# Selective-scan head loop of a macaron layer: each VectorE instruction waits for the matmul it needs instead of for the end of TensorE's slot

## The reference

```
x = x + 0.5 * ffn(layernorm(x))
x = x + attn(layernorm(x))          # attn: res + mamba2(ln1), then res + gelu-MLP(ln2)
x = x + 0.5 * ffn(layernorm(x))

# in mamba2: 32 heads of 64 channels, state 64 x 64 per head
def step(h, inp):
    x_t, dt_t, B_t, C_t = inp
    dA = exp(dt_t * A)
    h = h * dA[:, :, None, None] + (dt_t[:, :, None] * x_t)[..., None] * B_t[:, None, None, :]
    y = einsum('bhpn,bn->bhp', h, C_t)
    return (h, y)
y = ys + xs * D;  y = y * silu(z);  y = rmsnorm(y) * norm_w;  y @ out_proj_w.T
```

## Time and profile before

| quantity | value |
|---|---|
| median of four runs | 9365.92 us |
| the four runs | 9269.44, 9272.82, 9459.03, 9481.4 us |
| the profiled execution, its own time | 9273.08 us |
| span of its slowest core (core 3) | 9271.5 us |
| spans of the eight cores | 9232.7 to 9271.5 us |
| mean granted TensorE clock, as a share of 2.4 GHz | 0.710 to 0.711 on every core |

### The profile page before, as it was taken

How to read it: one execution, slowest core, us unless ns; L and a number is a source line. 1 busy time by engine, 2 the same in 40 slices (tenths; PEclk the granted TensorE clock), 3 DMA queues, 4 the chain that set the end, 5 groups by cost and what they waited for, 6 DMA issues and landing times.

```text
span 9271.5 us, 108299 instructions; the slowest of 8 cores (9232.7 to 9271.5 us)
## 1 busy us (share of the span) xinstructions
PE 5135.0 (55%) x22944; PEld 2260.1 (24%) x22944; DVE 4583.0 (49%) x12271; ACT 1898.0 (20%) x3892; POOL 60.0 (1%) x117
## 2 busy tenths in 40 slices
PE   0068888434434434335235335334337898888888
PEld 0023333212111212112112112112113343333333
DVE  2046656455555554554654654554552221365555
ACT  0023333211211211211112112112112222233332
POOL 1000000000000000000000000000000000000000
PEclk6589999655655656556557556556558999999999
DMA  9953433100100101001002002002004444434444
GB/s 184 204 147 117 126 121 117 58 1 12 52 1 23 40 1 37 27 1 57 7 1 63 1 1 63 1 1 63 1 1 125 136 134 137 125 121 130 129 127 126
DMA packets 191391, 653.06 MB, mean 70 GB/s; under 512 B 21296, under 2 KB 46128, under 8 KB 179504
## 3 DMA queue, kind: packets, MB, share of 16 engines
q1 hardware_dynamic: 174624, 590.46, 20.4%
q0 software_dynamic: 16176, 55.66, 4.1%
HBM read 629.62 MB, written 72.09 MB: 76 GB/s over the span
## 4 chain that ended last, share of the span: by engine, by line
PE 38%; DVE 35%; issue 14%; DMA 7%; ACT 3%; DVEq 2%; SPq 0%; ACTq 0%; POOL 0%; POOLq 0%
PE ps L242 38%; DVE arena L578 4%; DVE arena L573 4%; DVE arena L986 4%; DVE arena L769 4%; DVE hstate L997 3%; DVE arena L582 3%; DVEq L92 2%; DVE arena L960 2%; DVE arena L947 2%; DVE arena L968 2%; DVE arena L1072 1%; DMA cffn<-arena 1%; DMA arena<-wffn 1%; DMA arena<-wm 1%
## 5 line engine op out<-in xcount | busy, mean ns | idle before, releaser
L242 PE MATMUL ps<-arena,wk 128*128 128x512 f16 x15552 | 3542.7, 387 | 1080.2 <-DMA wk<-cffn 502.9
L242 PEld LDWEIGHTS ps<-arena,wk 128*128 128x128 f16 x15552 | 1511.9, 99 | 3103.7 <-issue 1436.5
L242 PE MATMUL ps<-arena 128*64 128x128 f16 (+1 forms) x1568 | 455.0, 290 | 1654.1 <-DVE arena L986 1311.5
L1010 ACT ACTIVATE arena<-arena 128x128 f32<-128x128 f32 x1024 | 316.5, 309 | 2762.4 <-DVE arena L947 2762.4
L947 DVE TENSOR_SCALAR arena<-ps,arena 128x128 f32<-128x128 f32 x1024 | 359.2, 351 | 853.6 <-PE ps L242 774.3
L573 DVE SCALAR_TENSOR_TENSOR arena<-arena,prm,ps 128x512 f32<-128x512 f32 x512 | 382.2, 747 | 636.8 <-ACT arena L571 547.7
L242 PEld LDWEIGHTS ps<-arena 128*64 128x64 f16 (+1 forms) x1568 | 198.7, 127 | 1917.7 <-issue 1859.1
L242 PE MATMUL ps<-arena,ind 32*128 32x128 f16 x3072 | 484.7, 291 | 283.1 <-issue 133.0
L568 ACT ACTIVATE arena<-ps,prm 128x512 f32<-128x512 f32 x512 | 351.9, 687 | 526.7 <-DVE arena L578 518.0
L578 DVE SCALAR_TENSOR_TENSOR arena<-arena,prm 128x512 f32<-128x512 f32 x512 | 384.4, 751 | 54.0 <-DVE arena L573 0.9
L249 PE MATMUL ps<-iden,arena 32*128 32x32 f32 x96 | 15.9, 287 | 703.5 <-DVE arena L811 703.5
(11 more groups left out here) (117 smaller groups left out, 3458.7 us busy)
## 6 DMA issues: line engine op xcount, KB each, us to landing
wk<-cffn SPq DMA_DIRECT2D x512, 512.0 KB, 3.9
wk<-cm SPq DMA_DIRECT2D x256, 512.0 KB, 3.7
wk<-cip SPq DMA_DIRECT2D x136, 512.0 KB, 3.6
wk<-cop SPq DMA_DIRECT2D x64, 512.0 KB, 3.8
arena<-wffn POOLq DMA_DIRECT2D x16, 1024.0 KB, 15.0
cffn<-arena SPq DMA_DIRECT2D x16, 1024.0 KB, 9.2
arena<-wm POOLq DMA_DIRECT2D x16, 1024.0 KB, 12.9
cm<-arena SPq DMA_DIRECT2D x16, 1024.0 KB, 4.8
```

Source lines behind the costliest of these rows:

```text
L242: e.matmul(a, l, r, start=st, stop=sp, tile_position=tp),
L1010: sD[s] = B.E("s", lambda e, s=s: e.activation(Dex[s % 2], e1[s % 2], AF.Exp), waits=[(s_v, ve1[s])], inc=s_s)
```

## The change

TensorE's counter is noted at four more places: after D(s) as `tD[s]`, after the transpose as `tTR[p]`, after Y(hh) as `tY[hh]` and after H(p) as `tH[p]`. VectorE's instructions no longer wait for `tslot[s]` but for the value that belongs to what they read. Where an instruction overwrites a buffer that an earlier matmul reads, and `tslot` had covered this, a wait for that matmul is added. Two waits of TensorE's transposes for `dx` of the chunk before are new as well. No engine's instructions change their order or their number, waits apart.

```diff
+                        tD[s] = s_t.n
...
+                        elif vdx_prev.get(p + 14) is not None:
+                            w0.append((s_v, vdx_prev[p + 14]))
                         t_tr(pbk, p16[p % 2][:, 0:128], xbc[p][:, qo:qo + 128],
                              iden16[:, :], waits=w0, inc=s_t)
+                        tTR[p] = s_t.n
...
+                        tY[hh] = s_t.n
...
+                            tH[p] = s_t.n
                     tslot[s] = s_t.n
...
                         bk = s % 2
-                        w0 = [(s_t, tslot[s]), (s_s, sv1)]
+                        w0 = [(s_t, tD[s]), (s_s, sv1)]
                         if s >= 2:
                             w0.append((s_s, sD[s - 2]))
                             w0.append((s_v, vG[s - 2]))
...
+                        w0 = [(s_t, tD[s])]
+                        if s >= 2:
+                            w0.append((s_t, tY[s - 2]))
                         vCd[s] = B.E("v", lambda e, bk=bk, s=s, qo=qo: e.tensor_tensor(
                             Cd16[s % 2], xbc[17][0:64, qo:qo + 128], ps[bk][0:64, 128:256],
-                            ALU.mult), waits=[(s_t, tslot[s])], inc=s_v)
+                            ALU.mult), waits=w0, inc=s_v)
                     if s % 2 == 0 and s < 32:
                         p = s // 2
-                        w0 = [(s_t, tslot[s]), (s_s, sv3)]
+                        w0 = [(s_t, tTR[p]), (s_s, sv3)]
+                        if p >= 2:
+                            w0.append((s_t, tY[2 * p - 3]))
...
+                        w0 = [(s_s, sv2)]
+                        if p >= 2:
+                            w0.append((s_t, tH[p - 2]))
...
-                                waits=([(s_s, sv2)] if par == 0 else []), inc=s_v)
+                                waits=(w0 if par == 0 else []), inc=s_v)
...
+                        w0 = [(s_s, sD[hh]), (s_v, vsp)]
+                        if hh >= 2:
+                            w0.append((s_t, tY[hh - 2]))
                         vG[hh] = B.E("v", lambda e, hh=hh: e.tensor_tensor(
                             G16[hh % 2], Dex[hh % 2], spm, ALU.mult),
-                            waits=[(s_s, sD[hh]), (s_v, vsp)], inc=s_v)
+                            waits=w0, inc=s_v)
...
-                            ALU.mult, ALU.add), waits=[(s_t, tslot[s])], inc=s_v)
+                            ALU.mult, ALU.add), waits=[(s_t, tY[hh])], inc=s_v)
...
-                                    waits=([(s_t, tslot[s]), (s_s, svA)] if par == 0 else []),
+                                    waits=([(s_t, tH[p]), (s_s, svA)] if par == 0 else []),
...
+                vdx_prev = {14: vdx[14], 15: vdx[15]}
```

More of the change, by code:

```diff
@@ L780, in mamba_stage @@
             bc_done = max(conv_done[16], conv_done[17])
+            vdx_prev = {}
             for q in range(DBG_NQ[0]):
@@ L814, in mamba_stage @@
                 tma = t_tr(2, ps[2][:, 64:96], dtb[:, q * 128:(q + 1) * 128], iden32[0:32, 0:32], inc=s_t)
+                w0 = [(s_s, bc_done)]
+                if vdx_prev.get(14) is not None:
+                    w0.append((s_v, vdx_prev[14]))
                 tmb = t_tr(6, p16[0][:, 256:320], xbc[16][0:64, qo:qo + 128], iden16[0:64, 0:64],
-                           waits=[(s_s, bc_done)], inc=s_t)
+                           waits=w0, inc=s_t)
                 sv1 = B.E("s", lambda e: e.activation(nctm, ps[2][:, 0:32], AF.Copy),
@@ L846, in mamba_stage @@
                 tslot = {}
+                tD = {}
+                tTR = {}
+                tY = {}
+                tH = {}
                 vG = {}
```

## The result

The changed kernel is faster: its time is 0.9632 of that of the kernel before, with a 95% interval of 0.9528 to 0.9735, so by 2.7 to 4.7%. The profiled execution took 8911.04 us where that of the kernel before took 9273.08, which is 362 us less. The median of seven runs is 9031.03 us.

A forecast was written before the change was run, and what follows sets the result against it. No engine was full; VectorE's e1 waiting for TensorE in odd slots was the loss, VectorE the bound in even slots. Per pair 0.98 - 0.05 - 0.26 = 0.67 us, with small terms 334 us: 9273 to 8939, set at 8945, range 8790 to 9110.

The forecast's parts named there:

- The place of the gain: Odd slots: e1 no longer waits for TensorE's Y and H, so Cd starts 0.98 us earlier.
- The wait that takes its place: Odd slots: Cd waits for Y's second matmul and starts 0.11 us after it ends, with e1 filling the wait.
- A side reckoning: Odd-slot Cd could start at 3199.00 by TensorE and 3198.87 by VectorE, so TensorE is later by 0.13 us.
- The price of an added wait: VectorE's path: 0.07 us per wait, 0.05 where partly covered; the rival that they are hidden, about 8780 us, had 0.18.
- TensorE as the bound: Even slots: TensorE has some 0.8 us to spare; the rival that its chain takes over, about 9090 us, had 0.13.
- The sum: All 32 head loops: 10.4 us won per loop, 334 us in all, from 9273 to 8939 us.
- the terms for odd and even slots: Regular pair: 0.98 won and 0.05 added in odd slots, 0.26 added in even ones; 5.46 in place of 6.13 us.
- the start of each loop: Slot 2 of each head loop: e1 and the gap behind it move under Cd's wait, 0.6 us won in all.
- the 0.03 per pair: Head loop: charge for VectorE stalls of 0.35 us that partly fell free into the TensorE wait; 0.64 us net per pair.
- From the e1 of slot 30 on: Loop end: the last pair wins 0.64 us, and evac of head 31 waits for Y instead of H, 0.25 us.
- The clock: Head loop: granted clock stays at 0.50 with PE's share 47%; if it rose, 62 us less.
- The level of the forecast: Time set at 8945 us, from the profiled execution's 9273 less 334, though the four runs' median was 9366.

The follow-up runs named there:

- cd_three: The changed kernel with three buffers for Cd in place of two, so Cd needs no wait for Y; lowest time 8709.48 us.
- all_but_e1: The changed kernel with e1 alone put back on the end of TensorE's slot, all other finer and added waits kept; lowest time 9454.8 us.
- waits_doubled: The changed kernel with six more already satisfied waits in each even slot, two each before Cd, dxw and G; lowest time 9098.56 us.
- prune_three: The changed kernel with already passed waits left out on all engines in the whole program, plus three Cd buffers; lowest time 8330.09 us.

## Why the prediction was right or wrong

**The place of the gain** was right. It is the e1 of odd slots, and e1 alone: its wait of 1.20 us is gone, and the kernel with only that line changed has the whole gain (8880.61 us) while the one with all the rest has none (9454.8 us).

**The wait that takes its place** was right. Cd waits for Y's second matmul, at 0.12 after its end where I had 0.11, and the rest of the wait lies under e1. A side reckoning was off: I had TensorE later than VectorE by 0.13 at this Cd, with e1 starting at 3198.28, though evac ends at 3198.25 and the changed kernel starts e1 0.07 before that end. With e1 0.10 earlier the distance is 0.23, so more was left for cd_three to take. It did not enter the pair, since Cd goes by TensorE there.

**The price of an added wait** was right at 0.07 where it falls on VectorE's path: the gaps show it one by one, all_but_e1 shows the sum with the gain taken away (+0.38 per pair), and waits_doubled adds six at 0.068. The page "VectorE: DVE Perf Modes" of the Trainium skill, section "The DRAIN you can't avoid", says of eight copies in a row that a semaphore after each costs nothing extra. That does not carry over to waits ahead of short operations in this kernel, where each costs 0.07.

**TensorE as the bound:** it is not. In even slots Cd has 0.24 of idle time, which is its own wait and two more.

**The sum** was close: 334 us forecast and 362 measured between the two profiled executions, 356 of it in the head loops (3182 to 2826). The regular pair was 5.46 as forecast, so the terms for odd and even slots stand. Two small terms were undersized. One is the start of each loop. From e1 of slot 0 to Cd of slot 3, the kernel before takes 8.49 us in one loop and the changed one 6.40 in another; the means over all 32 loops are 8.20 and 6.50, 1.70 less:

```profile
3147.88 0.35 DVE L947 TENSOR_SCALAR arena<-ps,arena 128x128 f32<-128x128 f32 x1 [1.46 <-PE p L249]
...
3156.37 0.28 DVE L953 TENSOR_TENSOR arena<-arena,ps 64x128 f16<-64x128 f16 x1 [0.17 <-DVE arena L947]
```

```profile
3161.93 0.35 DVE L961 TENSOR_SCALAR arena<-ps,arena 128x128 f32<-128x128 f32 x1 [1.27 <-PE ps L242]
...
3168.33 0.28 DVE L970 TENSOR_TENSOR arena<-arena,ps 64x128 f16<-64x128 f16 x1 [0.37 <-PE ps L242]
```

My terms give 0.6 for slot 2 and 0.98 - 0.26 for slot 3, 1.32 in all. The 0.26 was wrong there: dx, dxw and G get their added waits only from the third pair or head on. Taken up to the e1 of slot 4, where my terms give 0.60 + 0.64 = 1.24, the loops are 1.65 shorter on average (10.17 to 8.52), which makes 13 of the 28 us missing.

The other is the 0.03 per pair that I charged for the gaps that are 0.35 longer. Over the thirteen pairs from slot 4 to slot 30 the mean went from 6.22 to 5.56, 0.665 less, as 0.98 - 0.31 without that charge: 11 us. From the e1 of slot 30 on, the loop gained 0.82 (8.37 to 7.55) where I had 0.64 + 0.25: 2 us less than forecast. The last 6 us lie outside the head loops, where I had put nothing; what made them was not traced.

**The clock** stayed at 0.50 in the loop. Over the stretches from the e1 of slot 2 to that of slot 30 PE is busy 45% of the time, for 40% before; I had 47%. The page "TensorE: Matmul & The Clock Gate" of the Trainium skill, section "Part 1: The HAM clock gate (the "warmup" mystery)", lets the clock follow how busy the array was just before, and the denser loop did not change it; nor did the densest one here, prune_three:

```profile
3080.00:3110.00 30.00, 16.37 (x84) 8.45 (x84) 24.32 (x96) 4.36 (x14) 0.00 (x0) 0.50 0.00 0
```

**The level of the forecast is the step that failed.** The prediction said of the medians that "a median of the changed kernel can be moved the same way", and still set 8945, 6 us above the 8939 of the sum, with an upper end of 9110. The median of the seven runs came to 9031, 86 us above the 8945; that lies within the range, but two of the seven lie above 9110. The kernel before moved too: its median, 9366 over the four runs that I had, is 9466.61 over all ten, 2.1% above the execution from which I subtracted. On that level the ratio 0.9632 gives 9466.61 x 0.9632 = 9118 us, outside the range. The four runs showed two at 9270 and two at 9470, so the spread of 2% was in view; the range took in the bounds of the mechanism and left out the spread of the machine. It was even drawn inside its own upper bound, 9126. The mechanism is not what failed: the ratio of the forecast to its own level, 8939 / 9273 = 0.9640, is the measured 0.9632 within its interval. Why the runs of one kernel lie so far apart was not tried.

## What to carry to other kernels

When engines synchronise by counters, ask of each wait which instruction's result it needs and what else the noted value covers. The one to free is the instruction that stands first behind a gap and needs nothing from it; here a single edited line held the whole gain. Then look at what stands next behind the same gap: with e1 free, the finer wait of Cd was worth 0.25 us a pair, as long as it replaced the coarse one and nothing was added. Give the others the coarse wait or none: a wait that is already satisfied cost 0.07 us on VectorE and 0.105 on TensorE in the head loop, with operations of 0.3 us, and dropping those that the engine had already passed took 8902 to 8424 us without touching the computation.

## What the runs showed of the hardware

- The price of a satisfied wait does not depend on its number: one, two and four behind a wait for the engine's own result gave 0.17, 0.24 and 0.38, and 0.10 with none. I had not expected six of them to add up so evenly (0.41 for six).
- An instruction of VectorE that does not wait for its neighbour's result can start 0.07 to 0.08 before the one ahead of it has ended (e1 at 3178.43 behind an evac that ends at 3178.50, evac at 3178.17 behind a G that ends at 3178.25).
- Some gaps are 0.35 longer than their fellows in all the kernels, as the earlier trace rows showed. Their places are regular: numbering VectorE's instructions in the trace from 0, waits included, all 365 such gaps found from slot 6 on, before e1, Cd, dxw and G of even slots on one core of each of the eleven traces, stand at a number that leaves 59 to 63 when divided by 128. The streams differ in length from 24822 to 37201 instructions. What makes them was not tried.
